# The four projections of an attention and mixing block with operands as scaled fp16 pairs

## What is computed

```python
x = x + layernorm(attn(layernorm(x)))
x = x + layernorm(ffn(layernorm(x)))

def attn(x):                     # one head of width 256
    qkv = x @ weight_qkv         # columns 0:64 and 192:256 of x in fp16, the middle in fp32
    q, k, v = split(qkv, 3);  q = q / sqrt(256)
    return (softmax(q @ k.T) @ v) @ out_w.T + out_b

def ffn(x):                      # x_prev is x one row earlier, zeros in front
    xr = mu_r * x + (1 - mu_r) * x_prev
    xk = mu_k * x + (1 - mu_k) * x_prev
    r = sigmoid(xr @ W_r.T)
    return r * (square(relu(xk @ W_k.T)) @ W_v.T)
```

## Time and profile before

| | us |
|---|---|
| median of 3 runs | 859.05 |
| lowest run | 858.09 |
| highest run | 1708.93 |
| the profiled execution | 856.61 |
| its span, first to last instruction | 854.8 |

### The profile page before, as it was taken

One profiled execution on the slowest core, in us unless ns is written; L12 is line 12 of the kernel. 1 busy time (PEld: TensorE's weight loads), 2 busy tenths in 40 slices (PEclk: granted clock), 3 DMA queues, 4 the chain that ended last, 5 costly groups with the idle time before them and its releaser, 6 DMA issues.

```text
span 854.8 us, 16115 instructions
## 1 busy us (share of the span) xinstructions
PE 809.6 (95%) x5870; PEld 614.0 (72%) x5870; DVE 693.6 (81%) x1767; ACT 503.1 (59%) x634; POOL 434.0 (51%) x638
## 2 busy tenths in 40 slices
PE   4779999999999999999999999999999999999963
PEld 3437777777777777777777777777777777778853
DVE  4687798877899888877988888888877777898683
ACT  3275566655566675655676756656766565566532
POOL 1100254655656566556546665564456555645872
PEclk8799999999999999999999999999999999999977
DMA  6568854546656646566455666675435455545301
GB/s 178 112 139 144 177 137 107 125 106 141 148 118 117 142 107 143 117 124 148 106 117 119 142 150 118 124 142 99 106 88 105 113 110 123 125 99 108 79 12 38
DMA packets 336574, 101.58 MB, mean 119 GB/s; under 512 B 310256, under 2 KB 336240, under 8 KB 336496
## 3 DMA queue, kind: packets, MB, share of 16 engines
q1 hardware_dynamic: 336496, 100.56, 54.8%
HBM read 18.75 MB, written 8.39 MB: 32 GB/s over the span
## 4 chain that ended last, share of the span: by engine, by line
PE 88%; DVE 5%; POOL 2%; ACT 1%; issue 1%; DMA 1%; SPq 1%; ACTq 0%; POOLq 0%; DVEq 0%
PE M L885 7%; PE M L886 7%; PE M L887 7%; PE S L917 6%; PE Y L936 6%; PE Y L939 6%; PE Y L937 6%; PE Y L938 6%; PE Y L940 6%; PE S L921 6%; PE S L918 6%; PE S L920 6%; PE S L919 6%; PE M L965 2%; DMA xs<-in_L_attn_x 1%
## 5 line engine op out<-in xcount | busy, mean ns | idle before, releaser
L681 DVE TENSOR_SCALAR_CACHE_REDUCE probs<-S 128x512 f32<-128x512 f32 x256 | 173.0, 679 | 94.9 <-PE S L921 94.4
L514 ACT ACTIVATE probs<-probs,exp_bias,kappa 128x2048 f32<-128x2048 f32 x64 | 134.0, 2094 | 70.7 <-DVE exp_bias L692 70.7
L697 DVE TENSOR_TENSOR p_lo<-probs,p_hi 128x2048 f16<-128x2048 f32 x64 | 166.0, 2594 | 1.9 <-ACT p_hi L475 1.9
L936 PE MATMUL Y<-pt_hi,planes 128*128 128x256 f16 x512 | 139.6, 273 | 0.3 <-issue 0.3
L939 PE MATMUL Y<-pt_lo,planes 128*128 128x256 f16 x512 | 139.6, 273 | 0.0
L937 PE MATMUL Y<-pt_lo,planes 128*128 128x256 f16 x512 | 139.6, 273 | 0.0
L940 PE MATMUL Y<-pt_hi,planes 128*128 128x256 f16 x512 | 139.6, 273 | 0.0
L938 PE MATMUL Y<-pt_hi,planes 128*128 128x256 f16 x512 | 139.6, 273 | 0.0
L475 ACT ACTIVATE p_hi<-probs 128x2048 f16<-128x2048 f32 x64 | 122.0, 1906 | 1.2
L917 PE MATMUL S<-turned,q_hi 128*128 128x512 f16 x256 | 98.8, 386 | 10.3 <-DVE probs L681 7.7
L532 ACT ACTIVATE att<-att,ashift,arstd 128x256 f32<-128x256 f32 x62 | 33.9, 593 | 111.6 <-POOL ashift L387 111.6
(11 more groups left out here) (135 smaller groups left out, 2078.9 us busy)
## 6 DMA issues: line engine op xcount, KB each, us to landing
x_res<-in_L_attn_x SPq DMA_DIRECT2D x32, 256.0 KB, 3.8
out_x<-gate SPq DMA_DIRECT2D x32, 256.0 KB, 3.0
xs<-in_L_attn_x SPq DMA_DIRECT2D x32, 128.0 KB, 3.1
xs<-in_L_attn_x SPq DMA_DIRECT2D x16, 256.0 KB, 4.0
pt_hi<-p_hi SPq DMA_TRANSPOSE x64, 4.5
pt_lo<-p_lo SPq DMA_TRANSPOSE x64, 3.7
pt_hi<-in_L_attn_weight_qkv SPq DMA_DIRECT2D x3, 128.0 KB, 2.8
pt_hi<-in_L_attn_weight_qkv SPq DMA_DIRECT2D x1, 256.0 KB, 3.1
```

The lines of the kernel that those rows point to most:

```text
L681: dve.tensor_scalar(probs[:, t, c * BLK:(c + 1) * BLK], S[k % RING][:, :], 1.0, None, ALU.mult, ALU.max, accum_out=chunk_max[:, t, c:c + 1 ...
L697: dve.tensor_tensor(p_lo[:, t, :], probs[:, t, :], p_hi[:, t, :], ALU.subtract).then_inc(p_lo_made, 1)
L936: pe.matmul(to[:, 0, :], low, p_h, start=first, stop=False, skip_group_check=True)
```

## The change

All operands of the four projections (`wt_hi`, `wt_lo`, `y_hi`, `y_lo`, `xm_hi`, `xm_lo`, `sq_hi`, `sq_lo`) become fp16. As fp16 has a narrow range, they are scaled: the weights by 2^15 over the greatest absolute value of each matrix, the attended rows by 2^-26, the mixed rows by 2^11 over (1 + greatest mu), the squares by a factor from the norm of the rows of W_k. The factors are taken from the weights in the start: VectorE takes the maxima per partition (`peaks_of`, slot 4), ScalarE the sums of squares (slot 3), PE turns the [128, 7] tile (slot 6), VectorE takes the maximum of each and puts it on a diagonal (slot 8), PE spreads it to all partitions (slot 9), VectorE inverts (`tops`, slot 9), GpSimd works out the factors (`scales`, slot 9). High and low parts of the weights move to slots 11 and 13 and to 12 and 14. The slots of the stages stay.

```diff
-        wt_hi = sb("wt_hi", [P, 4, HALVES, D], F32R)
+        wt_hi = sb("wt_hi", [P, 4, HALVES, D], F16)
...
-        QK_BANK, FOLD_BANK, PEAK_BANK = Y[1], Y[0], M[0]
-        TURN_BANKS = [S[0], S[1], S[2], M[2], M[1], M[2], Y[1]]
+        QK_BANK, FOLD_BANK, PEAK_BANK = Y[1], M[2], M[0]
+        TURN_BANKS = [S[0], S[1], S[2], M[2], M[1], Y[1], Y[0]]
@@ gpsimd @@
+            def scales():
+                pool.wait_ge(top_made, 1)
...
+                pool.tensor_tensor(inv_row[:, :], row_square[:, :], minus_half[:, 0:1], ALU.pow).then_inc(inv_row_made, 1)
...
             for k in range(SLOTS):
+                if k == 9:
+                    scales()
@@ scalar @@
+            def row_norms_of():
+                act.wait_ge(w_in, (len(STAGED) - 1) * 16)
+                for e in range(HALVES):
+                    act.activation(square[:, e, :], stage_w[:, KEY, e], ACT.Square,
+                                   accum_out=peaks[:, ROW_0 + e:ROW_0 + e + 1]).then_inc(row_norms, 1)
+            def keep_val():
+                act.wait_ge(w_turned, 7)
+                copy(relu[:, :, :], pair(TURN_BANKS[6][:, :])).then_inc(val_kept, 1)
             def weight_high(i):
+                w, from_ = WEIGHTS[i]
+                act.wait_ge(weight_scale_made, 1)
+                act.activation(wt_hi[:, w], folded(from_), ACT.Identity,
+                               scale=weight_scale_of[:, w:w + 1]).then_inc(w_hi_made, 1)
-                copy(y_hi[:, :, :], pair(Y[h % 2][:, :])).then_inc(y_hi_made, 1)
+                copy(y_hi[:, :, :], pair(Y[h % 2][:, :]), 2.0 ** -(P_EXP + X_EXP)).then_inc(y_hi_made, 1)
-                copy(xt[:, h % 2, :, 1:ROWS + 1], pair(TURN_BANK[:, :])).then_inc(xt_made, 1)
+                act.activation(xt[:, h % 2, :, 1:ROWS + 1], pair(TURN_BANK[:, :]), ACT.Identity,
+                               scale=mix_scale[:, 0:1]).then_inc(xt_made, 1)
-                act.activation(rec[:, :, :], pair(REC_BANK[:, :]), ACT.Tanh, scale=0.5).then_inc(rec_made, 1)
+                act.activation(rec[:, :, :], pair(REC_BANK[:, :]), ACT.Tanh,
+                               scale=rec_scale[:, 0:1]).then_inc(rec_made, 1)
-                act.activation(square[:, :, :], relu[:, :, :], ACT.Square).then_inc(sq_made, 1)
+                act.activation(square[:, :, :], relu[:, :, :], ACT.Square, scale=key_scale[:, 0:1]).then_inc(sq_made, 1)
...
                 if k == 3:
-                    weight_high(0, out_multiplied, 1)
-                    weight_high(1, w_turned, 5)
-                if k == 5:
-                    weight_high(2, w_turned, 6)
-                    weight_high(3, w_turned, 7)
+                    row_norms_of()
+                    keep_val()
+                if k in (11, 13):
+                    weight_high(k - 11)
+                    weight_high(k - 10)
@@ vector @@
+            def peaks_of():
+                dve.wait_ge(w_in, (len(STAGED) - 1) * 16)
+                dve.tensor_reduce(peaks[:, KEY:VAL + 1], stage_w[:, KEY:VAL + 1].rearrange("p w h c -> p w (h c)"), AX.X,
+                                  ALU.max, apply_absolute_value=True).then_inc(peaks_made, 1)
...
+            def diagonal_of_peaks():
+                dve.wait_ge(peaks_turned, 1)
...
+            def tops():
+                dve.wait_ge(peaks_spread, 1)
...
+                dve.scalar_tensor_tensor(out=y_lo[:, :, :], in0=pair(Y[h % 2][:, :]), scalar=2.0 ** -(P_EXP + X_EXP),
+                                         in1=y_hi[:, :, :], op0=ALU.mult, op1=ALU.subtract).then_inc(y_lo_made, 1)
             def inverse_sums(h):
-                dve.reciprocal(inv_sum[:, h % 4, :], row_sum[:, h % 4, :]).then_inc(inv_made, 1)
+                dve.reciprocal(inv_sum[:, h % 4, :], row_sum[:, h % 4, :]).then_inc(sum_inverted, 1)
+                dve.wait_ge(sum_inverted, h + 1)
+                dve.tensor_scalar(inv_sum[:, h % 4, :], inv_sum[:, h % 4, :], top[:, OUT:OUT + 1], None,
+                                  ALU.mult).then_inc(inv_made, 1)
                 if k == 4:
-                    weight_low(0)
-                    weight_low(1)
-                if k == 6:
-                    weight_low(2)
-                    weight_low(3)
+                    peaks_of()
+                if k == 8:
+                    diagonal_of_peaks()
+                if k == 9:
+                    tops()
+                if k in (12, 14):
+                    weight_low(k - 12)
+                    weight_low(k - 11)
@@ tensor @@
                 if k == 2:
                     multiply_weights(2, 3, FOLD_BANK, out_multiplied)
                     pe.wait_ge(w_in, (len(STAGED) - 1) * 16)
-                    turn_weight(4)
-                if k == 4:
-                    turn_weight(5)
-                    turn_weight(6)
+                    for i in range(4, 7):
+                        turn_weight(i)
+                if k == 6:
+                    pe.wait_ge(peaks_made, 3)
+                    pe.wait_ge(row_norms, HALVES)
+                    pe.wait_ge(q_lo_made, begun(k, QUERY))
+                    pe.transpose(PEAK_BANK[0:PEAKS, 0:P], peaks[:, :], ident[:, :]).then_inc(peaks_turned, 1)
+                if k == 9:
+                    pe.wait_ge(diag_made, 1)
+                    pe.matmul(PEAK_BANK[:, 0:PEAKS], twos[0:PEAKS, :], peak_diag[:, :], start=True,
+                              stop=True).then_inc(peaks_spread, 1)
```

More of the change, by code:

```diff
@@ L192, in pair, with folded @@
             return ap.rearrange("p (t d) -> p t d", t=2)
+        def folded(tile):
+            return tile[:, :, :] if tile is relu else pair(tile[:, :])
         def unit(h, u):
@@ L439, in squares_low @@
                 pool.wait_ge(sq_hi_made, h + 1)
-                pool.tensor_tensor(sq_lo[:, :, :], square[:, :, :], f32(sq_hi[:, :, :]), ALU.subtract).then_inc(sq_lo_made, 1)
+                pool.tensor_tensor(sq_lo[:, :, :], square[:, :, :], sq_hi[:, :, :], ALU.subtract).then_inc(sq_lo_made, 1)
             def finish(h):
@@ L485, in weight_turned, with weight_high @@
                 copy(turned_w[:, i], pair(TURN_BANKS[i][:, :]), scale).then_inc(w_copied, 1)
[L487 to L490, removed]
+            def row_norms_of():
[6 more added lines that the diff above has]
+                copy(relu[:, :, :], pair(TURN_BANKS[6][:, :])).then_inc(val_kept, 1)
+            def weight_high(i):
+                w, from_ = WEIGHTS[i]
+                act.wait_ge(weight_scale_made, 1)
+                act.activation(wt_hi[:, w], folded(from_), ACT.Identity,
+                               scale=weight_scale_of[:, w:w + 1]).then_inc(w_hi_made, 1)
             def qk_high():
@@ L575, in _ @@
             qk_high()
[L576 removed]
+            weight_turned(2)
             weight_turned(3)
@@ L664, in weight_low @@
             def weight_low(i):
-                w, from_, scale = WEIGHTS[i]
+                w, from_ = WEIGHTS[i]
                 dve.wait_ge(w_hi_made, i + 1)
-                dve.scalar_tensor_tensor(out=wt_lo[:, w], in0=pair(from_[:, :]), scalar=scale, in1=f32(wt_hi[:, w]),
-                                         op0=ALU.mult, op1=ALU.subtract).then_inc(w_lo_made, 1)
+                dve.scalar_tensor_tensor(out=wt_lo[:, w], in0=folded(from_), scalar=weight_scale_of[:, w:w + 1],
+                                         in1=wt_hi[:, w], op0=ALU.mult, op1=ALU.subtract).then_inc(w_lo_made, 1)
@@ L781, in split_low @@
                     dve.wait_ge(xm_hi_made, h * 2 + i + 1)
-                    dve.tensor_tensor(xm_lo[:, i], mixed[:, i], f32(xm_hi[:, i]), ALU.subtract).then_inc(xm_lo_made, 1)
+                    dve.tensor_tensor(xm_lo[:, i], mixed[:, i], xm_hi[:, i], ALU.subtract).then_inc(xm_lo_made, 1)
             def squares_low(h):
@@ L786, in squares_low @@
                 dve.wait_ge(sq_hi_made, h + 1)
-                dve.tensor_tensor(sq_lo[:, :, :], square[:, :, :], f32(sq_hi[:, :, :]), ALU.subtract).then_inc(sq_lo_made, 1)
+                dve.tensor_tensor(sq_lo[:, :, :], square[:, :, :], sq_hi[:, :, :], ALU.subtract).then_inc(sq_lo_made, 1)
             def finish(h):
```

107 lines of the change are left out of this document (91 added, 16 removed).

## The result

| | before | after |
|---|---|---|
| median | 858.57 us (856.3 to 859.05, and one run of 1708.93; 4 runs) | 848.17 us (846.25 to 848.42, 4 runs) |
| profiled execution, its span | 856.61, 854.8 us | 847.97, 846.2 us |
| one block of eight slots, middle | 24.55 us | 24.135 us |

One run of before took twice the time of the others and enters no comparison. The ratio of the others is 0.9891, with a 95% interval of 0.9873 to 0.9908: 1.1% faster, certain as a difference and inside the 2% that one measurement of this kernel tells. The forecast was 851.4 us with a range of 845.0 to 860.5. The profiled execution lost 8.6 us of time and 8.6 us of span, where the sum had -7.6.

What follows compares the result with a forecast made beforehand. PE's matmul starts were taken to pace the 32 blocks, VectorE and ScalarE to lead the start. Terms: -11.3 + 0.7 + 3.0 = -7.6 us, giving 849.0 profiled, 851.4 median; range 845 to 860.5.

Steps and rivals of the forecast that it cites:

- part 1: Projection matmuls in the blocks: fp16 brings starts to 0.109 us apart, saving 0.39 us a block, -11.3 us over 29 blocks.
- tail: Last blocks' projections: scale tiles lengthen squares and turned copy on the chain, +0.7 us (-1 to +5); half-clock matmuls gain nothing.
- start: Slots before the blocks: finding scales at run time delays VectorE and PE, +3.0 us (bounds +1 to +7).
- rival d: Projections: weight loads bind after all and halving them gives part of 152 us; 820 for a quarter; chance 0.03.
- I give nothing: Projections: shorter weight loads, 197 to 98 ns, credited with no time, as loads already lie beside matmuls.
- Rival (c): Projections: the 8 ns per matmul come from bank or order, not type; only costs stay, 862.8 us; chance 0.08.
- Part 2: Per-block work on ScalarE, VectorE and GpSimd: dearer operations, covered under PE in the blocks; +0.7 us in the tail.
- rival (b): GpSimd's subtractions with fp16 operands are slow, at 5.5 us making PE wait each block: +50 us, 901; chance 0.03.
- The walk through VectorE: Start, slots 4 to 11: added operations and the wait for the diagonal shift VectorE +0.9, then +2.7, scores 14 +2.9 us.
- From there PE leads again: Start, from scores 14: low weight parts at slots 12 and 14 delay VectorE 2.4 us, within its margin until slot 23.
- Rival (a): Start, slots 6 to 11: waits drop the clock and block 1 waits for low halves; 11.5 to 15 us, 861; chance 0.08.
- My correction for turning all weights at slot 2: Start: turning all three weights at slot 2 takes eight transpositions out of slot 4, 0.9 us or less.

Runs made afterwards that it cites:

- e7: Kernel before, fp32r, with each projection matmul split into two of 128 columns; start unchanged: 1021.5 us, one execution.
- e1: Changed kernel with its eight operand tiles set back to fp32r, scales, start and order kept: 862.69 us, ratio 1.0069 to the kernel before.
- e8: Changed kernel with receptance and keys in fp32r, output and feed still fp16: 854.28 us, one execution, beside 856.25.
- e2: Changed kernel with constant scales, no run-time scale finding, weight parts back at slots 3 to 6: 842.44 us, ratio 0.9833.
- e3: Changed kernel with high weight parts all at slot 11 and low ones at slots 19 and 21: 847.81 us, ratio 0.9897.
- e9: Changed kernel with spread matmul behind slot 10's scores, weight parts at slots 11, 19, 21, maxima at slot 7: 844.79 us, ratio 0.9857.

## Why the prediction was right, point by point

| step of the prediction | forecast | measured |
|---|---|---|
| per block, part 1 | -0.39 us (0.33 to 0.43) | -0.413 |
| blocks in which it counts | 29, -11.3 us | 26 in full, -10.75; -0.18 and -1.23 at the two ends |
| tail | +0.7 us | -0.02 |
| start | +3.0 us (+1 to +7) | +2.32 at slot 16; +5.35 beside e7's start |
| sum | -7.6 us | -8.6 |

**Part 1 was right, in its place and its size.** The distance of starts, not the durations and not the load times, gave the time: 0.109 us for each of the 12 starts of a group, in all four groups. e1 shows that the type alone makes it (24.55 to 24.135 in the same order), e8 that it adds by groups, and PE waited for nothing between 64 and 785 us, as forecast. I was 6% under, by stamps of 0.01 us. The weight load as a price to be added (rival d) fell: no 152 us, nor a quarter. But its mechanism is real: e7 shows that the fp32r matmul is held by something other than its columns. It simply stands only 3 to 8 ns above the column stream at 256 columns, and the fp16 stream takes over at 0.109. "I give nothing" for the shorter loads was right in the sum and wrong as a reason: the 8 ns are very likely the load.

**Rival (c) fell** with e1: the 8 ns are a matter of type.

**Part 2.** The scale tiles: 92, 92, 92 and 89 ns against 93 taken. GpSimd's small operations ended at 56.97, as reckoned near 57.5, though most took 0.19 us, the pow 0.55 and one 2.18; and 1160 and 1292 ns for the fp16 subtractions against 1.29 us taken, so rival (b) had no room. The second operation of the inverse sums was mis-sized: 0.43 us on average in place of 0.16, 0.65 in 15 of the 32 blocks and about 0.23 in the others (the last section shows by what). It cost nothing; VectorE stayed under PE at 89.2 of 100 us, as reckoned (89.5).

**The tail is the term that failed in its parts.** I took +0.7 us from scale tiles and gave the half-clock matmuls nothing. Up to the feed projection of block 29 the fp16 form gave 1.23 us (e1 63.59 us from slot 248, after 62.36), and the run-time scales cost 0.25 (e1 against before) to 0.49 (after against e2, 61.87): net -0.98. Behind that point 33.8 us remain in the kernel after, 32.85 before, 35.6 in e1 and 31.7 in e2, and e3 with the same code as the kernel after differs by 1.1 us. Where PE waits, the granted clock of a window of 10 us is anything from 0.50 to 0.98 (both in e2, 820 to 840 us), differently in each execution. The 96.17 against 96.19 is thus a gain of 0.98 and a loss of 0.96, and what part of the loss is the scale tiles and what part the clock stays open.

**The start: near in sum, by luck.** The +2.32 beside the profiled execution of before is near the +3.0, but only because that execution had lost 3.03 us of its own by slot 16, as e7 shows: 0.2 ahead of 35 us, 1.7 in the stretch at the 1.2 GHz level from 36 to 40 us, and 1.2 in scores 14 and 15 at that level. Beside e7, which ran at full clock from 30 to 70 us, the new start can be followed step by step:

| by then | forecast | after, less e7 |
|---|---|---|
| first p_lo | +0.9 | +0.91 (46.97, 46.06) |
| second p_lo | +2.7 | +3.76 (54.08, 50.32) |
| scores 14 | +2.9 | +4.03 (59.18, 55.15) |
| scores 16 | +3.0 | +5.35 (64.06, 58.71) |

The walk through VectorE was right: what is over in the second and third rows, 1.1 us, is scores 10 at half clock (51.11 to 53.22 in place of 1.08 us), which I had named and not counted. Against it I set scores 14 and 15 at full clock, which is a matter of the execution too (0.61 in before, 0.39 in e7 and in the kernel after). Then the step that failed: "From there PE leads again", with the weight_low at slots 12 and 14 "inside the margin". The margin that I named was that of the projections at slot 23, and I did not look at what stood behind the moved work in VectorE's order: the low query part, which PE's slot 16 waits for. PE stood 1.46 us for it, and e3 shows it by removing it (slot 16 -1.40). Rival (a) had this mechanism at a later place and with too high a price. So at a like clock the term of the start was under-sized by 2.35 us. With +5.35 in its place the sum is -5.3 and the median forecast 853.8, still inside the range.

My correction for turning all weights at slot 2 ("0.9 us or less") is not borne out: e2 has it and e7 has not, and VectorE's fourth slot starts at 37.55 in both.

**The range** has a slip. The tail's own upper bound was +5 us, the sum of the bounds took +2; with +5 the upper end is 861.6, above the 860.5 stated. The measured 848.17 is far from it.

**The median** fell by 10.4 us (858.57 to 848.17), the profiled execution by 8.6. The 18 like runs of before, those beside the experiments included, lie between 853.5 and 859.1, a scatter that slow stretches like the 3.03 us of one start can make. So the verdict stands on the interval, the blocks on the spans, and of the two ends only differences above that are certain.

## What to carry to other kernels

In a kernel paced by matmul starts, read the price of an operand type as the distance between starts at the actual column count; the load time says only at how many columns it will begin to bind. At 256 columns fp32r lost 7% to fp16 here, at 128 a factor of two, so fp32r operands should not be cut into narrow matmuls. When work is moved within an engine's hand-written order, list what stands behind it there and who waits for each item, not only when the moved result is wanted; and put reductions that nobody waits for into a stretch where the engine is idle, as e9 does. In a stretch with many waits, gains of single stops do not add, since the clock granted there may take one back. And before a difference in such a stretch is credited to an edit, look for another execution with the same code there, whatever else that run changed, and compare the granted clocks: here that decided two readings, of the moved turns and of the lock.

## What the runs showed of the hardware that I had not expected

- VectorE and GpSimd hold each other up where VectorE's operation has two operands in SBUF, and it is the second to come that waits. GpSimd's scale chain is mostly a row of operations of 0.19 us. In the kernel after, one of 2.18 us is a plain 128x1 multiplication: it begins 0.15 us behind VectorE's p_lo (54.08) and ends at 56.41, when p_lo has ended. In e9 the same multiplication takes 0.19, and an operation of the chain that took 0.19 in the kernel after, and now begins 0.03 us behind p_lo (50.73), takes 2.30. Beside VectorE's score copy, which reads one operand from PSUM (53.46 to 54.15), the operations at 53.54 and 53.69 stay at 0.19 and 0.20. The timelines of GpSimd, of the kernel after and then of e9:

```profile
54.23 2.18 POOL L431 TENSOR_TENSOR feed_scale<-feed_scale 128x1 f32<-128x1 f32 x1
```

```profile
50.76 2.30 POOL L415 TENSOR_SCALAR mix_scale<-inv_top 128x1 f32<-128x1 f32 x1
```

- The other way round, this is the price of the second operation of the inverse sums, which I had at 0.16 us. It takes 0.65 where GpSimd's gate operation began 0.10 us ahead of it, and 0.23 where none did. The timeline of both engines at 448 us, and at 422 us of the same kernel:

```profile
448.27 1.41 POOL L507 TENSOR_TENSOR gate<-gate,res 128x256 f32<-128x256 f32 x2
448.37 0.65 DVE L812 TENSOR_SCALAR inv_sum<-inv_sum,top 128x2 f32<-128x2 f32 x1
```

```profile
422.90 0.23 DVE L812 TENSOR_SCALAR inv_sum<-inv_sum,top 128x2 f32<-128x2 f32 x1
```

  That the two engines share their way into SBUF is the likeliest reading; no run took the partner away alone. The Trainium skill (GPSIMD Engine Reference, Specifications) says that GpSimd's SBUF interfaces are shared with VectorE, with contention where VectorE is in a mode that uses two ports or has two SBUF inputs; these rows agree, and which of the two conditions holds for the small operation isn't shown.

- The first fp32r matmul behind a row of fp16 ones has 0.20 us to the next start, but starts only 0.03 us behind the last fp16 one (415.59, 415.62, 415.82), so the pair takes no longer than two steps of 0.117.
